# Moving the y sums of the output projection's seven products from GpSimd to VectorE, behind each head's gate

## The chip, the cores and the metric

One core of a Trainium2 chip runs the whole program. The metric is the time of one execution on the device, in microseconds (us); lower is better. Engine names in the profile: PE is TensorE (PEld its weight loads), DVE is VectorE, ACT is ScalarE, POOL is GpSimd, SP is SyncE.

## The reference, cut to what matters

1024 tokens (4 sequences of 256) with 512 features pass through a linear-attention layer with 32 heads of 128, a gate and an output projection, then a layer norm, then a small mixture layer with a second layer norm.

```python
qkv = silu(x @ qkv_w.T)                      # 32 heads, q, k, v of 128 each
# per head: decayed linear attention in blocks of 32
out = cq @ ck.T * diag_decay @ cv + (cq * q_decay) @ kv
attn = out                                   # [tokens, 32 * 128]
normed = norm_w * attn * rsqrt(mean(attn ** 2) + EPS)
gate = sigmoid(x @ gate_w.T)
x = layernorm(x + (gate * normed) @ out_w.T)
x = layernorm(x + ffn(x))                    # base, router and 8 low-rank experts
```

The change touches only how `(gate * attn) @ out_w.T` gets its operands. Call `y` the gated attention output of four heads.

## The kernel before, in words

The 32 heads are worked in 8 groups of four. Every float32 product is made as three products of fp32r pieces: an operand is split in a high part, written by ACT, and a low part, full minus high, written by DVE. The large projections (q and k, values, gate, output) use a scheme of seven block products in place of eight, named 1 to 7 in the code, so sums and differences of blocks have to be made ahead of them: of weights (`sums`, POOL) and of activations.

For the output projection of a group the operands come from `y`, a tile of four heads by 1024 tokens, cut in blocks `y11`, `y12`, `y21`, `y22` (two heads by 512 tokens each). Products 1, 2 and 4 take blocks as they are. Products 5, 6, 7 and 3 take sums:

- product 5: `y_temp = y21 - y22`
- product 7: `y21 - y11`, written over `y21`
- product 6: `y11 - (y21 - y22)`, written over `y11`
- product 3: `y12 - y11`, with `y11` as product 6 has it, written over `y_temp` (the tile `y_home`)

`y_sums(g, k)` makes the first three for head k of each pair (k = 0, 1), three instructions of 128x512; `y_last_sum(g)` makes the fourth. The operands are ready when `gated` (L1271, DVE) has multiplied a head's attention output, which lies in PSUM, by its gate.

For group g from 1 to 7 the program passes through the stages `qk0`, `v0`, `v1` and `output`, in which the last two heads of group g-1 are finished, the weights and values of group g are projected, and the output projection of group g-1 is added; then come `g01`, `qk1`, `g23`, `qk2`, `qk3`. The instruction order on each engine is written out by hand, one function for each stage and engine. Each engine works through its list in order and waits on semaphores. Where the text speaks of group 3, this is g = 3, whose window lies at 337 to 391 us; the last two heads are h-2 and h-1 with h = 4g.

Names and lines that the prediction uses:

- DVE: `gated` L1280, `add_part` L1268 (adds a piece to the attention output before its square), `mask` L1251 and L1253, `mask_sum` L1259, `scores_lo` (the rows `s<-ps,s` of L1179), `sums_lo` (the rows `wl<-stage,wh` of L1179), `c22_add` L1209, `c12_add` L1218, `y_sums` L1901 to L1906 and `y_last_sum` L1915 (on POOL before).
- ACT: `square` L629, `part`, `scores_hi`, `u3_copy` and `scale_rows` (all rows of L471), in the order of the stage functions: in `v1` that is `part(h-1,1)`, `u2_copy`, `square(h-1,1)`, `sums_hi(oa,A)`, `v21_out`, `p5_copy`, `operand_hi(5)`, `scores_hi(h,0)`, `u3_copy`.
- POOL: `sums` L1884, L1887, L1891, `add_squares` L1927.
- PE: `attention` starts at L2007 and waits for `scores_lo`; `p7` (L2084) waits for `u3_copy` through `cp12`; `p4` (L2061) waits for `c22_add` through `c22_added`.

Of the kernel before, what the change touches and what calls it, by code (L numbers as in the profile page):

```python
# [20 lines left out]
HG = 4  # L21
# [46 lines left out]
OUT_SUMS = 8  # L68
# [58 lines left out]
def operand_no(g, i):  # L127

    return 7 * (g - 1) + OUT_ORDER.index(i) + 1
# [21 lines left out]
def build(nc, stream, xt, x, decay, norm_w, base_b, lora_router, router_b, expert_map, ident_in, ones_in, fresh_in, out):  # L151
    ctx = ExitStack()
    with ctx:
# [26 lines left out]
        y_temp = y_home[:, :, :]  # L180
# [995 lines left out]
        def _(dve):  # L1176
# [4 lines left out]
            def sums_lo(g, name, part):  # L1181
                m = load_no(g, name)
                dve.wait_ge(t_hi, part_no(g, name, part))
                u0, u1 = (0, 3) if part == "A" else (3, 7)
                runs = pieces(g, name, u0, u1)
                for i, (slot, before, n) in enumerate(runs):
                    ins = minus(wl[:, slot:slot + n, :], stage[:, m % 2, u0 + before:u0 + before + n, :],
                                wh[:, slot:slot + n, :])
                    if i == len(runs) - 1:
                        ins.then_inc(t_lo, 1)  # L1190
# [20 lines left out]
            def c12_add(n):  # L1211
                dve.wait_ge(p_done[3], n + 1)
                dve.wait_ge(cp5, n + 1)
                dve.wait_ge(c12_out, n)
                dve.wait_ge(k0_lo, heads_before(n))
                if n == block_no(GROUPS - 1, QK3):
                    dve.wait_ge(gate_done, 3)
                nc.vector.tensor_tensor(c12_pre, ps[:, B1, :], p5s, ALU.add).then_inc(c12_added, 1)  # L1218
# [25 lines left out]
            def mask(h, e):  # L1244

                i = 2 * h + e
                dve.wait_ge(sc_done, i + 1)
                if e == 0:
                    dve.wait_ge(dec_in[h % 2], 16 * (h // 2 + 1))
                dve.wait_ge(s_full, i)  # L1250
                nc.vector.tensor_tensor(ssum[:, :, :], att_banks(e, SC, W),  # L1251
                                        dec[:, h % 2, 0:P].unsqueeze(1).broadcast_to([P, 2, P]), ALU.mult)
                nc.vector.tensor_tensor(att_banks(e, 0, SC), att_banks(e, 0, SC),  # L1253
                                        dec[:, h % 2, :].unsqueeze(1).broadcast_to([P, 2, SC]), ALU.mult)\
                    .then_inc(s_parts, 1)
# [15 lines left out]
            def gated(h, e):  # L1271
                dve.wait_ge(sq_done, 2 * h + e + 1)
                n = block_no(h // HG, G01 if h % HG < 2 else G23)
                if e == 0 and h % HG % 2 == 0:
                    dve.wait_ge(c11_out, n + 1)
                    dve.wait_ge(c21_out, n + 1)
                    dve.wait_ge(c12_out, n + 1)
                    dve.wait_ge(c22_out, n + 1)
                dst = by_batch(y[:, h % HG, half(e)])
                nc.vector.scalar_tensor_tensor(out=dst, in0=dst, scalar=1.0, in1=att_banks(e, 0, SEQ),  # L1280
                                               op0=ALU.add, op1=ALU.mult).then_inc(y_done, 1)

            def operand_lo(g, i):

                dve.wait_ge(y_hi, operand_no(g, i))
                hi, lo = y_operand[i]
                if i in (1, 2, 4):
                    ins = nc.vector.scalar_tensor_tensor(out=lo, in0=y_full[i], scalar=-1.0, in1=f32(hi),
                                                         op0=ALU.mult, op1=ALU.subtract)
                else:  # L1290
                    ins = minus(lo, y_full[i], hi)
                ins.then_inc(y_lo, 1)
# [96 lines left out]
            def qk0(g):  # L1389
                n, h = block_no(g, QK0), HG * g  # L1390
                k0_low(n - 1, h - 1)
                add_part(h - 2, 0)
                q1_low(n - 1, h - 1)
                gated(h - 2, 0)
                k1_low(n - 1, h - 1)
                sums_lo(g, "vb", "A")
                add_part(h - 2, 1)
                gated(h - 2, 1)
                mask(h - 1, 0)
                c22_add(n)  # L1400
                mask_sum(h - 1, 0)
                sums_lo(g, "va", "B")
                c12_add(n)
                values_lo(h - 1)
                scores_lo(h - 1, 0)
                sums_lo(g, "vb", "B")

            def v0(g):
                n, h = block_no(g, V0), HG * g
                q0_low(n - 1, h)  # L1410
                mask(h - 1, 1)
                k1_low(n - 1, h)
                mask_sum(h - 1, 1)
                k0_low(n - 1, h)
                q1_low(n - 1, h)
                scores_lo(h - 1, 1)
                add_part(h - 1, 0)
                c22_add(n)
                gated(h - 1, 0)
                c12_add(n)  # L1420

            def v1(g):
                n, h = block_no(g, V1), HG * g
# [15 lines left out]
            def output(g):  # L1439
                h = HG * g  # L1440
                sums_lo(g, "oa", "B")
                sums_lo(g, "ob", "B")
                operand_lo(g, 7)
                operand_lo(g, 2)
                out_add(g, "p5", 0)
                out_add(g, "c11", 0)
                out_add(g, "p5", 1)
                out_add(g, "c11", 1)
                operand_lo(g, 3)
                out_add(g, "c22", 0)  # L1450
                operand_lo(g, 4)
                out_add(g, "c22", 1)
                sums_lo(g, "g01", "A")
                out_add(g, "c12", 0)
                sums_lo(g, "g01", "B")
                out_add(g, "c12", 1)
                values_lo(h)
                out_add(g, "c21", 0)
                out_add(g, "c21", 1)
# [386 lines left out]
        def _(pool):  # L1846
# [44 lines left out]
                nc.gpsimd.tensor_tensor(stage[:, s, 6, :], stage[:, s, 2, :], stage[:, s, 3, :], ALU.add)\  # L1891
                    .then_inc(t_sum, 1)

            def y_sums(g, k):

                h = HG * g
                made = OUT_SUMS * (g - 1) + 3 * k
                pool.wait_ge(y_done, 2 * (h - 2 + k) + 1)
                if k == 0 and g > 1:
                    pool.wait_ge(y_lo, operand_no(g - 1, 3))  # L1900
                nc.gpsimd.tensor_tensor(y_temp[:, k, :], y21[:, k, :], y22[:, k, :], ALU.subtract).then_inc(y_sum, 1)  # L1901
                nc.gpsimd.tensor_tensor(y21[:, k, :], y21[:, k, :], y11[:, k, :], ALU.subtract).then_inc(y_sum, 1)
                pool.wait_ge(y_sum, made + 2)
                if k == 0:
                    pool.wait_ge(y_lo, operand_no(g, 1))
                nc.gpsimd.tensor_tensor(y11[:, k, :], y11[:, k, :], y_temp[:, k, :], ALU.subtract).then_inc(y_sum, 1)  # L1906

            def y_last_sum(g):

                h = HG * g  # L1910
                pool.wait_ge(y_sum, OUT_SUMS * (g - 1) + 6)
                pool.wait_ge(y_done, 2 * (h - 1) + 2)
                pool.wait_ge(y_lo, operand_no(g, 5))
                for k in range(2):
                    nc.gpsimd.tensor_tensor(y_temp[:, k, :], y12[:, k, :], y11[:, k, :], ALU.subtract).then_inc(y_sum, 1)  # L1915

            def next_sums(g, name):
                if g + 1 < GROUPS:
                    sums(g + 1, name)
# [18 lines left out]
            for g in range(GROUPS):  # L1938
                h = HG * g
                if g > 0:  # L1940
                    sums(g, "vb")
                    add_squares(h - 2, 0)
                    y_sums(g, 0)
                    add_squares(h - 2, 1)
                    sums(g, "oa")
                    add_squares(h - 1, 0)
                    y_sums(g, 1)
                    sums(g, "ob")
                    y_last_sum(g)
                    add_squares(h - 1, 1)  # L1950
                    sums(g, "g01")
                sums(g, "qk1")
                sums(g, "g23")
                if g == GROUPS - 1:
                    add_squares(h, 0)
                    sums(g, "qk2")
                    add_squares(h, 1)
                    sums(g, "qk3")
                    for hh in range(h + 1, HEADS):
                        add_squares(hh, 0)  # L1960
                        add_squares(hh, 1)
                    continue
                sums(g, "qk2")
                add_squares(h, 0)
                sums(g, "qk3")
                add_squares(h, 1)
                next_sums(g, "qk0")
                add_squares(h + 1, 0)
                next_sums(g, "va")
                add_squares(h + 1, 1)  # L1970
# [661 lines left out]
```

## Time and profile before

| what | value |
|---|---|
| median of 3 runs | 996.95 us (996.23 to 997.51) |
| the profiled execution, its own time | 996.55 us |
| its span from first to last instruction | 994.8 us |
| PE busy | 982.2 us, 99% of the span |
| DVE busy | 815.9 us, 82% |
| ACT busy | 710.0 us, 71% |
| POOL busy | 456.0 us, 46% |
| granted PE clock, mean | 0.998 |

Busy time says how full an engine is over the whole span. What a change is worth is read where one engine waits for another: for that the order in time of single instructions is needed, and the rows below give it for one group.

### The profile page before, as it was taken

Reading aid. Unit: us, or ns where it says so; the run is one execution under the profiler, and the core shown is the slowest. Engines: PE = TensorE matmul, PEld = TensorE weight load, DVE = VectorE, ACT = ScalarE, POOL = GpSimd, SP = SyncE. Lnnn points to the kernel's source line nnn. Section 1 sums busy time; section 2 is a strip of 40 time slices with the busy share of each in tenths; the row PEclk is TensorE's granted clock in tenths of the full one; section 3 lists DMA queues with packets and bytes.
Section 4 is the critical chain, followed back from the end, with each engine's and each line's share of the span. In section 5 each row is a group of like instructions: output and inputs, shape, how many; then the busy total and the mean of one; then the engine's idle time right before and its main releaser. Section 6 shows DMA issues by size and latency. Waiting matters only on the chain.

```text
span 994.8 us, 15911 instructions
## 1 busy us (share of the span) xinstructions
PE 982.2 (99%) x5569; PEld 860.6 (87%) x5569; DVE 815.9 (82%) x1122; ACT 710.0 (71%) x1197; POOL 456.0 (46%) x426
## 2 busy tenths in 40 slices
PE   8999999999999999999999999999999999999997
PEld 7878998889888898889988898888988899888896
DVE  6767887888967988779877889778887788899876
ACT  6677885788767785778857887677857788587653
POOL 1352564446453463534644464544635345531423
PEclk9999999999999999999999999999999999999999
DMA  6121111201121112212112111110122121110402
GB/s 211 30 64 46 64 48 48 71 30 52 51 65 51 35 47 72 63 44 66 45 55 66 30 52 51 64 51 30 51 72 64 38 73 38 56 52 22 159 12 85
DMA packets 52799, 57.78 MB, mean 58 GB/s; under 512 B 4336, under 2 KB 47728, under 8 KB 52720
## 3 DMA queue, kind: packets, MB, share of 16 engines
q1 hardware_dynamic: 52720, 56.77, 18.3%
q8 instruction: 45, 0.74, 0.3%
q14 instruction: 34, 0.28, 0.1%
HBM read 54.65 MB, written 2.10 MB: 57 GB/s over the span
## 4 chain that ended last, share of the span: by engine, by line
PE 93%; DMA 1%; ACT 1%; DVE 1%; issue 1%; POOL 1%; SPq 0%; POOLq 0%; ACTq 0%; DVEq 0%
PE ps L2013 25%; PE ps L2014 24%; PE ps L2015 24%; PE ps L2007 3%; PE ps L2009 3%; PE ps L2008 3%; PE ps L2110 2%; PE ps L2104 2%; PE ps L2106 2%; PE ps L2105 1%; PE ps L2124 1%; DMA stage<-stream 1%; PE ps L2108 1%; PE ps L2126 1%; DVE wl L1179 1%
## 5 line engine op out<-in xcount | busy, mean ns | idle before, releaser
L1884 POOL TENSOR_TENSOR stage<-stage 128x512 f32<-128x512 f32 x75 | 106.6, 1421 | 354.6 <-DMA stage<-stream 290.8
L2013 PE MATMUL ps<-xh,wh 128*128 128x512 f32 x658 | 260.0, 395 | 1.4 <-ACT stg L517 1.0
L2014 PE MATMUL ps<-xl,wh 128*128 128x512 f32 x658 | 257.0, 391 | 0.0
L2015 PE MATMUL ps<-xh,wl 128*128 128x512 f32 x658 | 256.2, 389 | 0.0
L1179 DVE TENSOR_TENSOR wl<-stage,wh 128x768 fp32r<-128x768 f32 (+3 forms) x183 | 201.3, 1117 | 28.4 <-ACT wh L471 27.7
L471 ACT ACTIVATE wh<-stage 128x768 fp32r<-128x768 f32 (+3 forms) x183 | 147.4, 833 | 17.8 <-POOL stage L1891 8.1
L2015 PEld LDWEIGHTS ps<-xh,wl 128*128 128x128 f32 x658 | 123.6, 188 | 26.8
L2013 PEld LDWEIGHTS ps<-xh,wh 128*128 128x128 f32 x658 | 123.7, 188 | 25.4 <-issue 1.8
L1927 POOL TENSOR_TENSOR sqacc<-sqacc,sq 128x512 f32<-128x512 f32 x64 | 92.8, 1451 | 110.9 <-ACT sq L629 110.9
L2014 PEld LDWEIGHTS ps<-xl,wh 128*128 128x128 f32 x658 | 123.7, 188 | 21.9
L471 ACT ACTIVATE ps<-ps 128x512 f32<-128x512 f32 x150 | 87.0, 584 | 65.0 <-PE ps L2015 65.0
L2013 PE MATMUL ps<-wh,xh 128*128 128x256 f32 (+1 forms) x423 | 122.8, 290 | 0.0
L2015 PE MATMUL ps<-wh,xl 128*128 128x256 f32 (+1 forms) x423 | 121.7, 288 | 0.0
L2014 PE MATMUL ps<-wl,xh 128*128 128x256 f32 (+1 forms) x423 | 121.5, 287 | 0.0
L1891 POOL TENSOR_TENSOR stage<-stage 128x256 f32<-128x256 f32 x75 | 81.0, 1080 | 5.9
L2013 PEld LDWEIGHTS ps<-wh,xh 128*128 128x128 f32 x423 | 80.8, 191 | 0.4
L2014 PEld LDWEIGHTS ps<-wl,xh 128*128 128x128 f32 x423 | 80.9, 191 | 0.3
L2015 PEld LDWEIGHTS ps<-wh,xl 128*128 128x128 f32 x423 | 80.8, 191 | 0.0
L1887 POOL TENSOR_TENSOR stage<-stage 128x256 f32<-128x256 f32 x75 | 68.4, 912 | 5.9
L1179 DVE TENSOR_TENSOR s<-ps,s 128x768 fp32r<-128x768 f32 x64 | 61.0, 953 | 10.1 <-ACT s L471 9.9
L471 ACT ACTIVATE s<-ps 128x768 fp32r<-128x768 f32 x64 | 51.7, 808 | 22.3 <-DVE ps L1259 22.2
L1253 DVE TENSOR_TENSOR ps<-ps,dec 128x768 f32<-128x768 f32 x64 | 61.1, 955 | 0.0
(224 smaller groups left out, 2320.9 us busy)
## 6 DMA issues: line engine op xcount, KB each, us to landing
stage<-stream SPq DMA_DIRECT2D x75, 384.0 KB, 3.4
stage<-stream SPq DMA_DIRECT2D x79, 128.0 KB, 2.1
dec<-decay SPq DMA_DIRECT2D x32, 192.0 KB, 2.4
stage<-stream SPq DMA_DIRECT2D x13, 256.0 KB, 3.1
acc<-xt SPq DMA_DIRECT2D x8, 256.0 KB, 6.0
v<-x SPq DMA_DIRECT2D x8, 256.0 KB, 5.8
out<-v SPq DMA_DIRECT2D x8, 256.0 KB, 2.0
y_home<-lora_router SPq DMA_DIRECT2D x1, 512.0 KB, 5.1
```

Of the source, the lines that this page charges most:

```text
L471: return nc.scalar.activation(dst, src, ACT.Copy, **kw)
L1179: return nc.vector.tensor_tensor(dst, full, f32(hi), ALU.subtract)
L1253: nc.vector.tensor_tensor(att_banks(e, 0, SC), att_banks(e, 0, SC), dec[:, h % 2, :].unsqueeze(1).broadcast_to([P, 2, SC]), ALU.mult)\
L1884: nc.gpsimd.tensor_tensor(stage[:, s, 1:5:3, :], stage[:, s, 0:6:5, :], stage[:, s, 7:8, :].broadcast_to([P, 2, U]), ALU.add).then_inc(t_p ...
L1887: nc.gpsimd.tensor_tensor(stage[:, s, 2, :], stage[:, s, 1, :], stage[:, s, 5, :], ALU.add)\
L1891: nc.gpsimd.tensor_tensor(stage[:, s, 6, :], stage[:, s, 2, :], stage[:, s, 3, :], ALU.add)\
L1927: nc.gpsimd.tensor_tensor(sqacc[:, e, :], sqacc[:, e, :], sq[:, :], ALU.add).then_inc(sq_added, 1)
L2007: nc.tensor.matmul(dst, wt[0], mv_[0], start=start, stop=False)
L2008: nc.tensor.matmul(dst, wt[0], mv_[1], start=False, stop=False)
L2013: nc.tensor.matmul(dst, wt[0], mv_[0], start=start, stop=False, skip_group_check=True)
L2014: nc.tensor.matmul(dst, wt[0], mv_[1], start=False, stop=False, skip_group_check=True)
L2015: return nc.tensor.matmul(dst, wt[1], mv_[0], start=False, stop=stop, skip_group_check=True)
```

## The change

The functions `y_sums` and `y_last_sum` move from the list of POOL to the list of DVE. Semaphores, operands and results are the same. The fourth sum becomes one instruction of 128x1024 in place of two of 128x512.

```diff
@@ VectorE: the functions, now here
+            def y_sums(g, k):
+                h = HG * g
+                made = OUT_SUMS * (g - 1) + 3 * k
+                dve.wait_ge(y_done, 2 * (h - 2 + k) + 1)
+                if k == 0 and g > 1:
+                    dve.wait_ge(y_lo, operand_no(g - 1, 3))
+                nc.vector.tensor_tensor(y_temp[:, k, :], y21[:, k, :], y22[:, k, :], ALU.subtract).then_inc(y_sum, 1)
+                nc.vector.tensor_tensor(y21[:, k, :], y21[:, k, :], y11[:, k, :], ALU.subtract).then_inc(y_sum, 1)
+                dve.wait_ge(y_sum, made + 2)
+                if k == 0:
+                    dve.wait_ge(y_lo, operand_no(g, 1))
+                nc.vector.tensor_tensor(y11[:, k, :], y11[:, k, :], y_temp[:, k, :], ALU.subtract).then_inc(y_sum, 1)
+            def y_last_sum(g):
...
+                dve.wait_ge(y_lo, operand_no(g, 5))
+                nc.vector.tensor_tensor(y_temp, y12, y11, ALU.subtract).then_inc(y_sum, 2)
@@ VectorE: qk0
                 gated(h - 2, 1)
+                y_sums(g, 0)
                 mask(h - 1, 0)
@@ VectorE: v0
                 gated(h - 1, 0)
                 c12_add(n)
+                y_sums(g, 1)
@@ VectorE: output
                 sums_lo(g, "oa", "B")
+                y_last_sum(g)
                 sums_lo(g, "ob", "B")
@@ GpSimd: group g > 0
                     sums(g, "vb")
                     add_squares(h - 2, 0)
-                    y_sums(g, 0)
                     add_squares(h - 2, 1)
                     sums(g, "oa")
                     add_squares(h - 1, 0)
-                    y_sums(g, 1)
                     sums(g, "ob")
-                    y_last_sum(g)
                     add_squares(h - 1, 1)
```

The end of stage `v0` and the start of `v1` on DVE before (the second `L1280` is the gate of the last head's second half, `L1251` opens `mask(h,0)`):

```order
L1209 TENSOR_TENSOR stg<-ps,stg 128x512
L1280 SCALAR_TENSOR_TENSOR y<-y,ps 128x512
L1218 TENSOR_TENSOR stg<-ps,stg 128x512
L1268 TENSOR_TENSOR ps<-ps,sq 128x2x128
L1280 SCALAR_TENSOR_TENSOR y<-y,ps 128x512
L1179 TENSOR_TENSOR wl<-stage,wh 128x768
L1251 TENSOR_TENSOR ssum<-ps,dec 128x256
```

The same place on DVE now (L1290, L1291 and L1295 are `y_sums`):

```order
L1209 TENSOR_TENSOR stg<-ps,stg 128x512
L1280 SCALAR_TENSOR_TENSOR y<-y,ps 128x512
L1218 TENSOR_TENSOR stg<-ps,stg 128x512
L1290 TENSOR_TENSOR y_home<-y 128x512
L1291 TENSOR_TENSOR y<-y 128x512
L1295 TENSOR_TENSOR y<-y,y_home 128x512
L1268 TENSOR_TENSOR ps<-ps,sq 128x2x128
L1280 SCALAR_TENSOR_TENSOR y<-y,ps 128x512
L1179 TENSOR_TENSOR wl<-stage,wh 128x768
L1251 TENSOR_TENSOR ssum<-ps,dec 128x256
```

The three sums stand between `c12_add` and `add_part(h-1,1)`; all that follows on DVE is behind them.

POOL at the same place before, from `add_squares(h-1,0)` to `add_squares(h-1,1)`:

```order
L1927 TENSOR_TENSOR sqacc<-sqacc,sq 128x512
L1901 TENSOR_TENSOR y_home<-y 128x512
L1902 TENSOR_TENSOR y<-y 128x512
L1906 TENSOR_TENSOR y<-y,y_home 128x512
L1884 TENSOR_TENSOR stage<-stage 128x2x256
L1887 TENSOR_TENSOR stage<-stage 128x256
L1891 TENSOR_TENSOR stage<-stage 128x256
L1915 TENSOR_TENSOR y_home<-y 128x512 x2
L1927 TENSOR_TENSOR sqacc<-sqacc,sq 128x512
```

And now (the lines are 25 or 2 further down in the changed file):

```order
L1929 TENSOR_TENSOR sqacc<-sqacc,sq 128x512
L1909 TENSOR_TENSOR stage<-stage 128x2x256
L1912 TENSOR_TENSOR stage<-stage 128x256
L1916 TENSOR_TENSOR stage<-stage 128x256
L1929 TENSOR_TENSOR sqacc<-sqacc,sq 128x512
```

The weight sums of `ob` follow `add_squares(h-1,0)` at once; before, three y sums stood between them.

## Rows read from the trace of the kernel before

**Rows 1.** Page, part 1: busy time of each engine, share, instructions.
```profile
PE 982.2 (99%) x5569; PEld 860.6 (87%) x5569; DVE 815.9 (82%) x1122; ACT 710.0 (71%) x1197; POOL 456.0 (46%) x426
```
**Rows 2.** Waits of PE: us in total, times, longest.
```profile
PE ps L2104 <- DVE y L1280: 0.2, 1, 0.2
```
**Rows 3.** Busy time by window: PE, PEld, DVE, ACT, POOL, clock, DMA.
```profile
337.00:372.00 35.00, 35.00 (x268) 33.78 (x268) 30.39 (x42) 29.12 (x53) 23.50 (x18) 1.00 0.12 38
```
**Rows 4.** Tile y_home on POOL: ns min/median/max, first and last start.
```profile
L1901 POOL TENSOR_TENSOR y_home<-y x14: 1290/1524/1766, 107.3 to 823.6; 128x512 f32<-128x512 f32 x14
...
L1915 POOL TENSOR_TENSOR y_home<-y x14: 1287/1304/1310, 135.1 to 833.8; 128x512 f32<-128x512 f32 x14
```
**Rows 5.** Timeline of DVE, group 3: start, us, line, operands, idle before.
```profile
338.30 1.29 DVE L1179 TENSOR_TENSOR k<-stg,k 128x512 fp32r<-128x512 f32 x1
339.51 2.05 DVE L1179 TENSOR_TENSOR wl<-stage,wh 128x768 fp32r<-128x768 f32 x1
...
342.57 0.69 DVE L1280 SCALAR_TENSOR_TENSOR y<-y,ps 128x512 f32<-128x512 f32 x1 [0.66 <-ACT sq L629]
...
353.57 0.69 DVE L1179 TENSOR_TENSOR q<-stg,q 128x512 fp32r<-128x512 f32 x1
354.87 0.96 DVE L1179 TENSOR_TENSOR s<-ps,s 128x768 fp32r<-128x768 f32 x1 [0.62 <-ACT s L471]
```
**Rows 6.** Timeline of POOL, group 3, around the first place.
```profile
337.74 1.30 POOL L1927 TENSOR_TENSOR sqacc<-sqacc,sq 128x512 f32<-128x512 f32 x1 [1.79 <-ACT sq L629]
339.00 1.75 POOL L1901 TENSOR_TENSOR y_home<-y 128x512 f32<-128x512 f32 x1
340.70 2.02 POOL L1902 TENSOR_TENSOR y<-y 128x512 f32<-128x512 f32 x1
...
355.66 0.74 POOL L1887 TENSOR_TENSOR stage<-stage 128x256 f32<-128x256 f32 x1
...
357.18 1.30 POOL L1927 TENSOR_TENSOR sqacc<-sqacc,sq 128x512 f32<-128x512 f32 x1
```
**Rows 7.** Timeline of DVE, group 3, the second place.
```profile
357.44 0.68 DVE L1218 TENSOR_TENSOR stg<-ps,stg 128x512 f32<-128x512 f32 x1
359.74 0.43 DVE L1268 TENSOR_TENSOR ps<-ps,sq 128x256 f32<-128x256 f32 x1 [1.61 <-ACT sq L471]
...
361.57 1.60 DVE L1179 TENSOR_TENSOR wl<-stage,wh 128x768 fp32r<-128x768 f32 x1
...
364.41 0.43 DVE L1259 TENSOR_TENSOR ps<-ps,ssum 128x256 f32<-128x256 f32 x1
...
368.94 0.69 DVE L1209 TENSOR_TENSOR stg<-ps,stg 128x512 f32<-128x512 f32 x1 [0.15 <-PE ps L2015]
```
**Rows 8.** Timeline of ACT, group 3.
```profile
356.70 1.70 ACT L471 ACTIVATE stage<-stage,nw 128x256 f32<-128x256 f32 x4
...
360.20 0.60 ACT L629 ACTIVATE sq<-ps 128x512 f32<-128x512 f32 x1
...
364.89 0.80 ACT L471 ACTIVATE s<-ps 128x768 fp32r<-128x768 f32 x1
365.58 0.60 ACT L471 ACTIVATE ps<-ps 128x512 f32<-128x512 f32 x1
```
**Rows 9.** Timeline of PE's weight loads, group 3.
```profile
356.46 0.19 PEld L2007 LDWEIGHTS ps<-s,vh 128*128 128x128 f32 x1
...
367.19 0.19 PEld L2013 LDWEIGHTS ps<-wh,xh 128*128 128x128 f32 x1
...
370.06 0.19 PEld L2013 LDWEIGHTS ps<-wh,xh 128*128 128x128 f32 x1
```
**Rows 10.** Group 6: DVE, then PE's weight load behind its last row.
```profile
688.28 3.21 DVE L1179 TENSOR_TENSOR wl<-stage,wh 128x512 fp32r<-128x512 f32 x2
...
704.74 0.96 DVE L1179 TENSOR_TENSOR s<-ps,s 128x768 fp32r<-128x768 f32 x1 [0.61 <-ACT s L471]
...
705.81 0.19 PEld L2007 LDWEIGHTS ps<-s,vh 128*128 128x128 f32 x1
```

More of the change, by code:

```diff
@@ L1281, in gated @@
                                                op0=ALU.add, op1=ALU.mult).then_inc(y_done, 1)
+            def y_sums(g, k):
[11 more added lines that the diff above has]
+            def y_last_sum(g):
+                h = HG * g
+                dve.wait_ge(y_sum, OUT_SUMS * (g - 1) + 6)
+                dve.wait_ge(y_done, 2 * (h - 1) + 2)
+                dve.wait_ge(y_lo, operand_no(g, 5))
+                nc.vector.tensor_tensor(y_temp, y12, y11, ALU.subtract).then_inc(y_sum, 2)
             def operand_lo(g, i):
@@ L1892, in sums @@
                     .then_inc(t_sum, 1)
[L1894 to L1915, printed above, removed]
             def next_sums(g, name):
```

## The prediction, made before the changed kernel ran

> **What bounds the kernel now.** I read the page's busy times first: PE is busy for 99% of the span, DVE for 82%, POOL for 46% [rows 1]. Then PE's waits: in the eight groups hardly any wait stands there, one of 0.2 us on the gate's row is the only one that a `y` instruction causes [rows 2]. Then the busy times by window: in group 3, from 337 to 372 us, PE is busy for all of 35.00 us at a granted clock of 1.00, while DVE has 30.39 us of work and POOL 23.50 [rows 3]. So PE sets the time. Work taken from POOL can't shorten it; work added to DVE costs nothing until one of its results comes after the moment at which PE wants it. From then on every us is lost for good, since PE has no gap to make it good in. The price of the change in a group is therefore the largest lateness, and not a sum of them.
>
> Last I read the single instructions in order of time, and there a second resource shows. A DVE instruction with two inputs in SBUF and 512 columns takes 0.69 us when POOL is idle (at 353.57 [rows 5]), but at 338.30 one took 1.29: POOL's `add_squares` ran from 337.74 to 339.04, and the DVE instruction ended 0.55 later [rows 5, 6]. The next, 768 wide, was issued at 339.51 and took 2.05, where an uncontended 768-wide one takes 0.96 (354.87); POOL's y sum of 339.00 had ended at 340.75, and it ended 0.81 later. POOL is held likewise: that y sum took 1.75 and the next one, behind the 768-wide instruction, 2.02, where 1.29 is the minimum [rows 4, 6]. With an input in PSUM nothing of this is seen: at 357.44, beside a POOL instruction of 357.18, DVE's add took 0.68 [rows 6, 7]. So the two engines exclude each other for whole instructions, and where both have a queue they alternate.
>
> The Trainium skill has this as a rule ("SBUF — State Buffer", section "Who interferes with whom"): a VectorE instruction with two SBUF inputs and a GpSimd instruction that reads SBUF take one shared port in turns, each for its whole length. The trace agrees, by the 1.29 and 2.05 us above. By that rule the sums below go through; without it they are those of the first rival.
>
> **What is removed, added and moved.** POOL loses eight instructions of 1.3 us a group, some 10.4 us, in seven groups [rows 4]. It isn't on PE's path, so this is worth nothing by itself. DVE gets six of 128x512 and one of 128x1024. The 512-wide ones have two SBUF inputs and cost 0.69 each, 0.6 from start to start, as successive rows overlap by 0.08 (338.30 + 1.29 = 339.59 against a start at 339.51 [rows 5]). Three with a semaphore wait between the second and the third are 1.9 us. The last sum, twice as wide, I put at 1.15. That is 5 us a group, 35 in all, without waits for POOL.
>
> First place, stage `qk0` (times are those of group 3). POOL's y sum no longer holds the 768-wide `sums_lo` of 339.51: it takes 0.95, so `add_part`, ACT's `square` and the gate come 1.10 earlier, the gate at 341.47 instead of 342.57 [rows 5]. The square's end also releases POOL's `add_squares`, 341.49 to 342.79. The first y sum, issued at 342.08, is held until 342.79 and ends at 343.34; the others follow, and DVE is free at 344.58. Before it was at 343.18 (342.57 + 0.61). Everything behind moves by 1.40 us.
>
> From here to 354 DVE and ACT feed each other without a gap: `mask`, `scores_hi`, `q0_low`, `q1_out`, `u3_copy`, `scale_rows`, `scores_hi`. So `scores_lo(h-1,1)`, which ran from 354.87 to 355.83, ends at 357.23 [rows 5]. PE loads the first weights of that attention at 356.46 [rows 9]. From the end of such a `scores_lo` to the load it releases 0.11 us pass, seen where PE did wait: 704.74 + 0.96 = 705.70, load at 705.81 [rows 10]. Lateness 357.34 - 356.46 = 0.88 us.
>
> Second place, end of `v0`. The gate of (h-1,0) is at 358.23, `c12_add` at 358.84 (357.44 + 1.40 [rows 7]), the y sums are issued from 359.44. ACT's `scale_rows(ob)`, 356.70 to 358.30 in steps before [rows 8], now ends at 359.80, and with no y sums in between POOL goes on to `sums(ob)` at once. So two queues meet. POOL `add_squares` 358.58 to 359.88; DVE's first sum held to it, ends 360.43; POOL L1884 ends 361.58 (1.15 behind it, as 340.75 stands to 339.59); second sum ends 362.13; POOL L1887 (0.74 alone [rows 6]) ends 362.73; third sum ends 363.28. The three take from 359.44 to 363.20, 3.8 us in place of 1.9. `add_part(h-1,1)` stood at 359.74 behind 1.61 us of idle time [rows 7]; it comes at 363.20, 3.46 later.
>
> What is late next. ACT's `square(h-1,1)` waits for `add_part` and goes from 360.20 to 363.65 [rows 8], and the whole ACT queue stands behind it. The gate comes at 364.28, `sums_lo(oa,A)` at 365.02, held until POOL's `add_squares` ends at 365.59, end 366.40; before it ended at 363.17, also held by a y sum (the 1.60 of 361.57 [rows 7]). `mask_sum(h,0)` moves from 364.41 to 367.65, ACT's `scores_hi` from 364.89 to 368.10, `u3_copy` from 365.58 to 368.80 with its end at 369.40. PE's `p7` loads at 367.19 [rows 9]: 369.50 - 367.19 = 2.3 us late. On DVE `c22_add` moves from 368.94 to 371.64, end 372.33; `p4` loads at 370.06 [rows 9]: 2.4 us late. The largest is what PE loses: 2.35 us a group.
>
> Third place, `output`. `y_last_sum` adds 1.15 us in front of `sums_lo(ob,B)` and operands 7 and 2. By then DVE is some 1.8 us behind its old times, and PE 2.35; with the sum it is 2.9 behind, and operand 2 had about 1 us to spare. I cost it at nothing; if that cover is gone, it is 0 to 0.5 us a group. It is likewise unknown whether the later POOL `sums(g01)` and `sums(qk1)` now hold operand 3: 0 to 0.4 us. I take zero, and keep both for the upper end.
>
> Sum: 7 x 2.35 = 16.4 us. In group 6 one piece of the cost is there already: its `sums_lo` stands in two instructions, 3.21 us with POOL's y sums between [rows 10], and PE came to the attention 17.53 us after it, in group 3 16.95 us (356.46 - 339.51). These 0.6 us go. That leaves 15.8. The profiled execution took 996.55 us (span 994.8 and 1.75 around it), so 1012.35; the median of the runs shown is 0.4 above it, 1012.8. I say 1012.5 us.
>
> Bounds. At the lower end the second place costs nothing more than the first: 0.88 a group. At the upper end PE gets the whole delay of `add_part`, 3.46 a group: 24 us.
>
> **Rivals.**
>
> *The first place alone counts.* If DVE's three sums go through back to back with POOL waiting, `add_part(h-1,1)` is at 361.35, 1.6 late, `u3_copy` ends at 367.8 and is 0.7 late, less than the 0.88 that PE has lost by then. 7 x 0.88 - 0.6 = 5.6 us: 1002.5 us. For it: the meeting with `sums(ob)` hangs on a few tenths of a us. Against it: in [rows 5, 6] the waiting POOL instruction got in between two DVE instructions that stood ready.
>
> *DVE's delay reaches PE whole.* If the operands of `output` are late as well, or the 1.0 us that `u3_copy` had is used up, PE loses 3.0 to 3.4 us a group, 21 to 24 us: 1019 us. For it: ACT's queue is strictly in order and carries every delay on. Against: DVE idles for 1.6 us at 359.74.
>
> *Cover holds.* DVE has 4.6 us free in the 35 us of [rows 3], about what is added. If the delay were taken up by idle time ahead of PE's loads, the time would be that of before, 997 us. Against: the idle time lies behind `scores_lo(h-1,1)`, and that one has only 356.46 - 355.83 - 0.11 = 0.5 us to spare.
>
> *Faster, by POOL's relief.* The held DVE instructions of 339.51 and 361.57 run free, PE's small waits of group 6 go, and DVE's results come earlier than before. It decides if the gate's gain of 1.10 exceeds the sums' cost, 2.5 with the hold. The price is what PE can win, the 0.6 us of group 6: 996.0 us, within the measurement. To be faster by 2 us there is no PE idle time in these stages [rows 3]. The Trainium skill ("GPSIMD Engine Reference", section "4.1 Engine selection") says that elementwise sums belong on VectorE, as GpSimd takes about twice as long; here it is 1.3 against 0.69 us, and the rule speaks of the engines' work, not of who is waited for.
>
> **How the numbers follow.** Main case 0.70 (own range 1007 to 1017), first place alone 0.12, whole delay 0.12, cover 0.04, faster 0.02. The range reaches into the first rival and the second: 1002 to 1019. A measurement can tell 0.2%, 2 us, from no change. Faster by more than that 0.02, within it 0.05, slower 0.93: only the cover case and a weak form of the first rival lie within 2 us.
>
> **What will show it.** PE's waits of the changed kernel: some 2.3 us a group, with ACT's copy into PSUM (`u3_copy`) or DVE's `c22_add` as releaser, in seven groups alike. The y sums on DVE: three of 0.7 us at best, the first held to 1.2, those of the second place 1.0, 1.8 and 1.1 long. POOL's L1884 row for `ob` starting between them. `sums_lo(vb,A)` down from 2.05 to 0.95. The prediction is wrong if PE's waits come from elsewhere, if the second place's sums run without a hold, or if PE's gaps sum to under 8 us. The granted clock should stay at 1.00, since the gaps are short.

## The result and the profile after

The changed kernel takes 1010.98 us (median of 4 runs, 1010.35 to 1011.92) against 996.96 us (4 runs). The ratio is 1.0144, with a 95% interval of 1.0132 to 1.0157: 14 us slower. Predicted were 1012.5 us in a range of 1002 to 1019.

Page of the changed kernel, part 1, beside [rows 1]:

```profile
PE 986.9 (98%) x5569; PEld 862.4 (85%) x5569; DVE 847.7 (84%) x1171; ACT 708.8 (70%) x1197; POOL 381.0 (38%) x370
```

DVE has 32 us more work, POOL 75 us less. PE runs the same 5569 instructions; its busy time reads 4.7 us more (986.9 for 982.2) because the ends of matmuls are modelled, so that a part of a gap counts as busy. PE's waits, beside [rows 2]:

```profile
PE ps L2012 <- ACT ps L471: 8.7, 9, 1.2
PE ps L2103 <- issue: 1.8, 5, 0.7
PE ps L2006 <- DVE s L1179: 1.8, 7, 0.3
...
PE ps L2012 <- DVE stg L1209: 0.5, 1, 0.5
```

Two waits are new, and each stands in all seven groups: seven of the nine on ACT's copy from PSUM to PSUM (1.15 to 1.22 us each, `u3_copy` of stage `v1`), and seven on DVE's `scores_lo`. These figures start where the last matmul is taken to end. The weight loads give the whole gap, and they show a third one that is too short to stand above. In group 3 of the changed kernel, which comes some 4.85 us later than before, three loads wait:

```profile
358.85 0.19 PEld L2012 LDWEIGHTS ps<-wh,xh 128*128 128x128 f32 x1 [0.35 <-ACT ps L471]
...
362.21 0.19 PEld L2006 LDWEIGHTS ps<-s,vh 128*128 128x128 f32 x1 [0.42 <-issue]
...
374.34 0.19 PEld L2012 LDWEIGHTS ps<-wh,xh 128*128 128x128 f32 x1 [1.36 <-ACT ps L471]
```

They are `p7` of `v0` (behind that stage's own `u3_copy`), the attention of (h-1,1) and `p7` of `v1`. I followed each product of PE through both traces: the distance to the old time grows by 0.39, 0.47 and 1.41 us at these three, 2.28 us in all over group 3. Over the seven windows it is 2.15, 2.28, 2.28, 2.21, 2.21, 1.77 and 1.86, in sum 14.8 us. Group 6 gives less, for the cost that it had before went away [rows 10].

DVE at the first place of the same group, beside [rows 5]:

```profile
344.35 0.95 DVE L1179 TENSOR_TENSOR wl<-stage,wh 128x768 fp32r<-128x768 f32 x1
345.22 0.42 DVE L1268 TENSOR_TENSOR ps<-ps,sq 128x256 f32<-128x256 f32 x1
346.30 0.69 DVE L1280 SCALAR_TENSOR_TENSOR y<-y,ps 128x512 f32<-128x512 f32 x1 [0.66 <-ACT sq L629]
346.90 1.28 DVE L1290 TENSOR_TENSOR y_home<-y 128x512 f32<-128x512 f32 x1
348.11 0.68 DVE L1291 TENSOR_TENSOR y<-y 128x512 f32<-128x512 f32 x1
348.83 0.69 DVE L1295 TENSOR_TENSOR y<-y,y_home 128x512 f32<-128x512 f32 x1
```

The 768-wide `sums_lo` fell from 2.05 to 0.95 us, and the first y sum took 1.28, held by POOL's `add_squares`. At the second place, DVE and then POOL, beside [rows 7] and [rows 6]:

```profile
364.30 0.96 DVE L1290 TENSOR_TENSOR y_home<-y 128x512 f32<-128x512 f32 x1
365.19 1.79 DVE L1291 TENSOR_TENSOR y<-y 128x512 f32<-128x512 f32 x1
367.01 1.11 DVE L1295 TENSOR_TENSOR y<-y,y_home 128x512 f32<-128x512 f32 x1
368.04 0.42 DVE L1268 TENSOR_TENSOR ps<-ps,sq 128x256 f32<-128x256 f32 x1
```

```profile
363.42 1.30 POOL L1929 TENSOR_TENSOR sqacc<-sqacc,sq 128x512 f32<-128x512 f32 x1
364.80 1.62 POOL L1909 TENSOR_TENSOR stage<-stage 128x512 f32<-128x512 f32 x1
366.50 1.06 POOL L1912 TENSOR_TENSOR stage<-stage 128x256 f32<-128x256 f32 x1
367.64 1.07 POOL L1916 TENSOR_TENSOR stage<-stage 128x256 f32<-128x256 f32 x1
```

Each DVE sum ends behind the POOL instruction that was under way, and each POOL instruction behind a sum: POOL's 363.42 + 1.30 = 364.72, the first sum ends at 365.26; L1909 ends at 366.42, the second sum at 366.98. From the first sum to `add_part` it is 3.74 us, and the lengths of the three sums are the same within 0.01 us in all seven groups. The next rows of ACT, beside [rows 8], carry it on:

```profile
368.49 0.60 ACT L629 ACTIVATE sq<-ps 128x512 f32<-128x512 f32 x1 [2.04 <-DVE ps L1268]
...
372.99 0.81 ACT L471 ACTIVATE s<-ps 128x768 fp32r<-128x768 f32 x1 [1.25 <-DVE ps L1259]
373.70 0.59 ACT L471 ACTIVATE ps<-ps 128x512 f32<-128x512 f32 x1
```

`u3_copy` ends at 374.29, and PE's load stands at 374.34.

### The profile page after: what moved, and what is told of

Its sections match the earlier page's. It is cut to its first block, busy times and chain, and to the rows that moved or that the text cites. A ratio compares the mean times of both kernels' runs of the same rounds, so it can differ in the third digit from the quotient of the medians.

```text
span 1010.1 us, 15911 instructions
## 1 busy us (share of the span) xinstructions
PE 986.9 (98%) x5569; PEld 862.4 (85%) x5569; DVE 847.7 (84%) x1171; ACT 708.8 (70%) x1197; POOL 381.0 (38%) x370
## 4 chain that ended last, share of the span: by engine, by line
PE 69%; DVE 14%; issue 6%; ACT 6%; DMA 2%; POOL 1%; SPq 0%; DVEq 0%; ACTq 0%; POOLq 0%
PE ps L2012 19%; PE ps L2013 18%; PE ps L2014 18%; DVE wl L1179 3%; PE ps L2006 3%; PE ps L2008 2%; PE ps L2007 2%; DVE y L1291 2%; DVE y_home L1290 2%; ACT sq L629 1%; DMA stage<-stream 1%; PE ps L2109 1%; DVE ps L1253 1%; ACT stage L471 1%; PE ps L2103 1%
## 5 line engine op out<-in xcount | busy, mean ns | idle before, releaser
L1909 POOL TENSOR_TENSOR stage<-stage 128x512 f32<-128x512 f32 x75 | 109.0, 1453 | 430.7 <-DMA stage<-stream 339.8
L1179 DVE TENSOR_TENSOR wl<-stage,wh 128x768 fp32r<-128x768 f32 (+3 forms) x183 | 185.1, 1026 | 27.7 <-ACT wh L471 27.1
L1916 POOL TENSOR_TENSOR stage<-stage 128x256 f32<-128x256 f32 x75 | 81.0, 1080 | 5.9
L1912 POOL TENSOR_TENSOR stage<-stage 128x256 f32<-128x256 f32 x75 | 71.0, 947 | 5.9
```

What stands on the lines that cost most here:

```text
L1179: return nc.vector.tensor_tensor(dst, full, f32(hi), ALU.subtract)
L1909: nc.gpsimd.tensor_tensor(stage[:, s, 1:5:3, :], stage[:, s, 0:6:5, :], stage[:, s, 7:8, :].broadcast_to([P, 2, U]), ALU.add).then_inc(t_p ...
L1912: nc.gpsimd.tensor_tensor(stage[:, s, 2, :], stage[:, s, 1, :], stage[:, s, 5, :], ALU.add)\
```

## The experiments

The theory: PE loses in each group what comes latest to it; DVE's delay comes from the added instructions and, more, from the port that DVE and POOL take in turns. The rivals: the loss follows the added DVE work; it lies in ACT's order; or it is the sum of separate prices. Each run is compared with runs of the kernel before on the same chip; the ratio is to these.

### One place at a time

In the first run k = 0 alone is on VectorE:

```diff
@@ GpSimd, against the changed kernel
                     add_squares(h - 1, 0)
+                    y_sums(g, 1)
                     sums(g, "ob")
+                    y_last_sum(g)
@@ VectorE: v0
                 c12_add(n)
-                y_sums(g, 1)
@@ VectorE: output
                 sums_lo(g, "oa", "B")
-                y_last_sum(g)
```

> Only the sums of qk0 (k = 0) are made by VectorE; those of v0 (k = 1) and the last sum stay on GpSimd. Theory (PE loses the largest lateness of a group; the first place gives 0.8 us, the second 1.4 more): 0.82 us a group, in two steps of 0.35 before p7 of v0 and 0.47 before the attention of (h-1,1), none before p7 of v1; group 6 gives 0.46 back: +5.3 us, 1002.3 us. Rival (the loss follows the VectorE work that is added, 35 us for 14): these are 13 of the 35 us, +5.2 us, 1002.2 us. This run alone doesn't part them by time; the place of PE's gaps does, since the rival has them wherever VectorE is late.

Measured: 1003.51 us against 996.76, ratio 1.0064 (1.0049 to 1.0079). Group 3 has the two first gaps and no third:

```profile
355.41 0.19 PEld L2035 LDWEIGHTS ps<-wh,xh 128*128 128x128 f32 x1 [0.35 <-ACT ps L471]
...
358.77 0.19 PEld L2029 LDWEIGHTS ps<-s,vh 128*128 128x128 f32 x1 [0.43 <-issue]
```

In groups 2 to 5 PE falls back by 0.77 to 0.85 us. The theory's 0.82 and its places are there. The loss of time is 6.8 us, and its interval, 4.9 to 7.9 us, holds the 5.3 that were expected. Group 7 loses 1.4, with a third gap at `p7` of `v1` that the theory did not have.

In the second run only `y_sums(g, 1)` stands in VectorE's list; `y_sums(g, 0)` and `y_last_sum(g)` are back on GpSimd.

> Only the sums of v0 (k = 1) are made by VectorE; those of qk0 and the last sum stay on GpSimd. Theory: VectorE reaches c12_add at its old time, the three sums meet GpSimd's add_squares and sums(ob), add_part(h-1,1) comes 2.1 us late, mask(h,0) 1.8 late, and the u3_copy's 1.0 us of slack leaves 0.9 us a group, all in one gap before p7 of v1: +6.2 us, 1003.2 us. With the first place's +5.3 that is 11.5, less than the 14.0 of both: a delay that is not used up at the first place eats the slack of the second. Rival (by VectorE work): 13 of 35 us, +5.2 us, and the two add up with the last sum to 14.

Measured: 1003.98 us, ratio 1.0071 (1.0055 to 1.0087). The three sums were held as expected (group 3, DVE):

```profile
361.15 0.98 DVE L1290 TENSOR_TENSOR y_home<-y 128x512 f32<-128x512 f32 x1
362.05 1.78 DVE L1291 TENSOR_TENSOR y<-y 128x512 f32<-128x512 f32 x1
363.87 1.11 DVE L1295 TENSOR_TENSOR y<-y,y_home 128x512 f32<-128x512 f32 x1
364.90 0.42 DVE L1268 TENSOR_TENSOR ps<-ps,sq 128x256 f32<-128x256 f32 x1
...
366.72 0.96 DVE L1179 TENSOR_TENSOR wl<-stage,wh 128x768 fp32r<-128x768 f32 x1
```

But PE's loss is 0.6 to 0.7 us a group, some 0.4 at `p7` of `v1` and 0.3 at the first output product, not 0.9 in one gap. I had let POOL's `add_squares(h-1,1)` hold the `sums_lo` of the last row. With `y_last_sum` still on POOL and waiting in front of it, POOL stands idle there, and the `sums_lo` took 0.96 us; in the changed kernel, where `y_last_sum` has left POOL, it is held:

```profile
369.85 1.43 DVE L1179 TENSOR_TENSOR wl<-stage,wh 128x768 fp32r<-128x768 f32 x1
```

In this run `add_squares` came later and held `sums_lo(ob,A)`. The seven windows account for some 5 of the 7.0 us by which the two profiled spans differ; 1.5 us lie ahead of group 1 and 0.6 between groups 2 and 3, and their cause is not known.

The time can't tell additive from not: this run and the one before give 6.8 and 7.2 us, with 0.7 of the next 14.7, near the 14.0 of the change, though each is known to 1.6 us only. In the traces the two places alone cost 0.8 and 0.6 to 0.7 us in an ordinary group, and together with the last sum 2.2. So they are not independent. The expectation had that direction, 11.5 for 14.0: the first place's delay is still on VectorE when the slack of `u3_copy` is used up. But this is not the whole excess of some 0.8 us. The 0.47 us by which `sums_lo(oa,A)` is held in the change and not here (1.43 against 0.96) comes from the last sum's leaving POOL. No run moves the second place and the last sum without the first, so the split between the two is read from rows and not measured by itself.

In the third run only `y_last_sum(g)` is on VectorE.

> Only the last sum (y12 - y11, 128x1024) is made by VectorE, y_sums stay on GpSimd. Theory: it is covered, PE loses nothing: 996.5 to 997.5 us, same as before. The sums_lo(ob,A) that was held by add_squares to 1.90 us runs elsewhere against GpSimd, since add_squares(h-1,1) comes 2.6 us earlier. Rival (by VectorE work): 8 of 35 us, +3.3 us, 1000.2 us.

Measured: 997.46 us, ratio 1.0011 (1.0001 to 1.0021). In groups 1 to 6 PE gains 0 to 0.3 us, group 7 loses 0.6. VectorE was given 1.1 us of instructions more a group, and only in group 7 did PE wait for it; VectorE's busy time grew by just 2 us over the kernel (817.9 for 815.9), since a hold fell away. `sums_lo(ob,A)` was no longer held (group 3, 0.95 for the 1.90 of before). The rival that goes by VectorE's work, as put at 1000.2 us, is out (the interval ends at 2.1 us, it wants 3.3).

### GpSimd waits, VectorE's work unchanged

```diff
@@ GpSimd, against the changed kernel
                     add_squares(h - 1, 0)
+                    pool.wait_ge(y_sum, OUT_SUMS * (g - 1) + 6)
                     sums(g, "ob")
```

> The changed kernel, and GpSimd waits with sums(ob) until VectorE has made the three sums of v0. Theory (the port held by whole instructions in turns is what makes the second place dear): the second and third sum on VectorE take 0.69 us each instead of 1.8 and 1.1, the three 2.3 us in place of 3.8; add_part(h-1,1) comes 1.9 late instead of 3.45, u3_copy is 0.7 late or less, under the 0.82 that PE has lost by then: 1.4 us a group less, 1002 us. Rival (the length of VectorE's queue and ACT's order alone): 1011 us as with the change, or later, since GpSimd's sums(ob) end later.

Measured: 1001.28 us, ratio 1.004 (1.0024 to 1.0056). One wait added, 10 us less. The sums of the second place in group 3:

```profile
362.33 0.96 DVE L1290 TENSOR_TENSOR y_home<-y 128x512 f32<-128x512 f32 x1
363.22 0.68 DVE L1291 TENSOR_TENSOR y<-y 128x512 f32<-128x512 f32 x1
363.93 0.69 DVE L1295 TENSOR_TENSOR y<-y,y_home 128x512 f32<-128x512 f32 x1
364.54 0.42 DVE L1268 TENSOR_TENSOR ps<-ps,sq 128x256 f32<-128x256 f32 x1
```

They take 2.21 us up to `add_part` in place of 3.74, and the 1.4 us gap is gone; 0.77 to 0.85 us are left in groups 2 to 5. This is the first rival of the prediction made true, DVE's three sums going through together, and the 1002.5 us that it gave is near.

The next run has this wait and a second one, `pool.wait_ge(y_sum, OUT_SUMS * (g - 1) + 3)`, ahead of `add_squares(h - 2, 1)`.

> The changed kernel, and GpSimd waits at both places until VectorE's three sums are made: with add_squares(h-2,1) at the first, with sums(ob) at the second. The work on both engines is that of the changed kernel. Theory: the first sum of qk0 takes 0.69 us instead of 1.28, mask(h-1,0) comes 0.8 late instead of 1.4, PE's gap before the attention of (h-1,1) shrinks from 0.82 in two steps to 0.25 in one, and nothing is late behind the second place: 1.8 us in seven groups less the 0.5 of group 6, 998.0 us (997 to 999.5). Rival (VectorE's queue is longer by 5 us a group, holds or not): no less than the run in which only sums(ob) waited, 1001.3 us.

Measured: 996.38 us against 996.39, ratio 1.0001 (0.9992 to 1.0009). All y sums are on VectorE, as in the changed kernel, and nothing is lost that the time can tell. The first sum took 0.68 us, and only one small gap is left in group 3:

```profile
342.99 0.68 DVE L1290 TENSOR_TENSOR y_home<-y 128x512 f32<-128x512 f32 x1
```

```profile
357.68 0.19 PEld L2008 LDWEIGHTS ps<-s,vh 128*128 128x128 f32 x1 [0.22 <-issue]
```

Groups 1 to 5 lose 0.10 to 0.23 us each, group 6 wins back 0.28: 0.7 us over the seven windows. The places were right, the size was not: the expectation had 1.3 us of loss and started from 996.7 us, the trace has 0.7, and the time shows none (its interval ends at 0.9 us). A rival by VectorE's busy time is out as well: it is 16 us above that of before (832.1 for 815.9) and costs nothing, where the 6 us more of the first run (821.8) cost 6.8. Some holds stay (the first sum of `v0` takes 0.97 us), and one that the kernel before had, on `sums_lo(vb,A)`, is gone, as with the change.

The first wait alone:

```diff
@@ GpSimd, against the changed kernel
                     add_squares(h - 2, 0)
+                    pool.wait_ge(y_sum, OUT_SUMS * (g - 1) + 3)
                     add_squares(h - 2, 1)
```

> The changed kernel, and GpSimd waits only at the first place (add_squares(h-2,1) behind VectorE's three sums of qk0); the second place keeps its meeting with sums(ob). Theory (largest lateness of a group): the first place's gap is 0.2 us, and since nothing else moves earlier than 0.6 us, u3_copy of v1 is 3.26 - 0.6 - 1.0 = 1.7 us late in all: 1.7 us a group, 11.9 less group 6's 0.5, 1008 us. Rival (the holds' costs add up, each wait takes away its own): the wait at the second place took 9.8 us of 14.1, this one takes the other 4.4, so 1006.4 us.

Measured: 1007.10 us against 996.27, ratio 1.0107 (1.009 to 1.0123). The interval, 9.0 to 12.3 us, holds both figures, so the time decides nothing. By the trace a group loses 1.54 to 1.69 us (groups 1 to 5), a gap of 0.2 and one of 1.41: 0.6 less than the change, which is the 0.6 that the hold of the first sum was worth. Here lateness and a sum of prices say the same.

### ScalarE's order

```diff
@@ ScalarE, stage v1, against the changed kernel
-                scores_hi(h, 0)
                 u3_copy(n)
+                scores_hi(h, 0)
                 sums_hi(g, "ob", "A")
```

> The changed kernel, and ScalarE does u3_copy of v1 ahead of scores_hi(h,0) instead of behind it. Theory: p7 of v1 is then on time, but VectorE's c22_add, which p4 of v1 waits for, is late by the same 2.2 to 2.3 us of a group (it ended at 377.21 in group 3, where p4's weight load would have come at 377.2 with the gap and 374.9 without it): PE's 1.4 us gaps move from ScalarE's copy to VectorE's add, the time stays at 1011 us (1010 to 1011.5). Rival (ScalarE's order behind square(h-1,1) is the cause): the gap of 1.4 us a group is gone, 1001 us.

Measured: 1012.04 us, ratio 1.0155 (1.014 to 1.017): 0.5 us above the range expected, and by its ratio not to be told from the change (1.0144). PE's waits:

```profile
PE ps L2012 <- DVE stg L1209: 8.4, 7, 1.3
PE ps L2006 <- DVE s L1179: 1.8, 7, 0.3
```

The wait on ACT's copy is replaced, seven times, by one on DVE's `c22_add`. In group 3 the instruction and the load behind it:

```profile
376.66 0.68 DVE L1209 TENSOR_TENSOR stg<-ps,stg 128x512 f32<-128x512 f32 x1
```

```profile
377.40 0.19 PEld L2012 LDWEIGHTS ps<-wh,xh 128*128 128x128 f32 x1 [1.39 <-DVE stg L1209]
```

Groups 1 to 5 lose 2.15 to 2.29 us each, as with the change. The releaser that a wait names need not be the cause; here two results were late by the same amount.

### GpSimd's order in the kernel before

```diff
@@ GpSimd, against the kernel before
                     add_squares(h - 2, 0)
-                    y_sums(g, 0)
                     add_squares(h - 2, 1)
+                    y_sums(g, 0)
                     sums(g, "oa")
```

> The kernel before, with GpSimd's y_sums(g,0) behind add_squares(h-2,1) instead of ahead of it; VectorE's list is unchanged. Theory: sums_lo(vb,A) is no longer held (0.95 us for 2.05), the gate comes 1.1 us earlier, and group 6, where the sums_lo in two pieces made PE 0.5 us late, loses this wait: 996.4 us, 0.5 under the kernel before, which the time can't tell but PE's waits can (none on the gate's row L1280). In the other groups nothing changes, since PE did not wait. Rival (GpSimd's order doesn't reach PE): PE's wait in group 6 stays.

Measured: 995.98 us against 996.39, ratio 0.9998 (0.9989 to 1.0006): no difference that can be told. `sums_lo(vb,A)` takes 0.94 us in group 3, group 6 wins 0.56 us and PE no longer waits on L1280, as the theory has it. What it has not is group 3, where PE loses 0.43 us at the attention of (h-1,1). The y sums, now later, meet the next `sums_lo`, of 256 and 768 columns, which took 1.28 us before:

```profile
345.33 3.37 DVE L1179 TENSOR_TENSOR wl<-stage,wh 128x256 fp32r<-128x256 f32 x2
```

Moving POOL's work moved the hold as well. The measurement doesn't show that this version beats the kernel before.

## Why the prediction was right, step by step

- **PE is full, so the latest result of a group sets the price.** Held. PE's gaps in the windows sum to 14.8 us of the 15.3 by which the two profiled spans differ. The rest lies at the start and the end.
- **First place.** Expected 0.88 us at the attention of (h-1,1); measured 0.39 + 0.47 = 0.86 in group 3. I had seen no lateness at `p7` of `v0`, though the same 1.40 us makes `u3_copy` late there too; it is a part of the 0.86, not more.
- **Second place.** Expected 3.8 us for three sums and `add_part` 3.46 us later; measured 3.74, and 368.04 - 4.85 - 359.74 = 3.45. Expected lengths 1.0, 1.8, 1.1; measured 0.96, 1.79, 1.11.
- **What is late next.** Expected `p7` 2.3 us late, `p4` 2.4; measured 2.28 in all at `p7`, and `p4` waits for no more than that. The term mis-sized is the 2.4: I had put 0.11 us between `c22_add` and PE's load, the trace has 0.05 (377.21 to 377.26), and 0.06 where PE did wait for it (377.34 to 377.40 with `u3_copy` first). 7 x 2.35 should have been 7 x 2.25. The other part of the error is that the run profiled of the changed kernel was the slowest of its four: medians differ by 14.0 us, profiled executions by 15.4.
- **Third place at nothing.** Held for VectorE's side: with the last sum alone on VectorE the ratio is 1.0011. Its leaving POOL is a part of the second place's price, by the hold on `sums_lo(oa,A)`; the prediction had counted that there (1.38 us, measured 1.43). The 0 to 0.9 us a group kept for it in the range were not needed.
- **Group 6.** Expected -0.6; its window lost 1.77 where the others lost some 2.2.
- **The rivals.** The whole delay did not reach PE, nor did cover hold, nor was relief of POOL a gain. What I had ranked too low is how much of the price is the port: the prediction's sum treats the added length and the holds alike, but with the two meetings taken away by waits and the same sums on VectorE nothing is left of the 14 us. The Trainium skill's rule ("SBUF — State Buffer", section "Who interferes with whom"), that a VectorE instruction with two SBUF inputs contends with a GpSimd instruction that reads SBUF, is the one on which the result hangs, and the trace agrees with it in every row shown, from the first sum's 1.28 us beside `add_squares` to its 0.68 us with POOL waiting.

What stays open: why groups 1 and 7 differ a little from the rest in several runs (2.15 and 1.86 with the change, 1.21 and 1.39 with the first place alone). Their `sums_lo` is cut in other pieces by the ring of weight slots; whether that is the reason is not shown, as no run tests it.

## What to carry to other kernels

When an engine is full, price a change at another engine by the latest result of each stage, and ask of every instruction that moves to VectorE with two SBUF inputs what GpSimd will be doing at that moment. Taking work from GpSimd lets its next work come earlier, and that can land on the very instructions that were moved: one wait on GpSimd, which had time to spare, was worth 10 us, two were worth all 14. Even so they only brought back the time of the kernel before: here the relief of an engine that PE did not wait for won nothing. A wait's releaser in the profile is the last link; look for a second one that is as late before reordering for the first.

## What the runs showed of the hardware that was not expected

In the rows of this case the turns are strict. Where both queues wanted the port they alternated instruction by instruction: the three POOL instructions of `sums(ob)` fell one by one between and behind three DVE sums whose own lengths are 0.69 us, and this in seven groups alike. A held sum of 512 columns ended 0.54 to 0.56 us behind the POOL instruction, some 0.14 us less than its own length. With two waits on POOL, some 5 us of VectorE instructions a group cost PE no more than 0.3 us in groups 1 to 6. The mean granted clock stayed at 0.997 to 1.000 in every run, also with gaps of 1.4 us in each group.
